# Two attention layers: head outputs compacted by DMA into two blocks of 96 rows, and maxima, exponentials and loads of x in other steps

## The chip, the cores and the metric

One core of a Trainium2 chip runs the whole program in one launch. The metric is device time in microseconds (us) from the program's start to its end. Engines that matter here: TensorE (PE, with its weight loads PEld), VectorE (DVE), ScalarE (ACT), GpSimd (POOL), and SyncE (SP), which issues the DMAs.

## What is computed

Four layers run one after the other on x of shape (16, 14, 14, 192): a GRU over the 196 positions, an attention layer (named l1 in the code), a layer of experts, and a second attention layer (l3). Each layer adds its output to its input, and its input is group-normalised first. Both attention layers have 12 heads of 16 channels, with a bias from relative positions, and differ in their weights only:

```python
q, k, v = (qkv[0], qkv[1], qkv[2])
attn = jnp.einsum('bqd,bkd->bqk', q * scale, k)
bias = rel_h[..., :, None] + rel_w[..., None, :]
attn = jax.nn.softmax(attn + bias.reshape(b * NH, h * w, h * w), axis=-1)
out = jnp.einsum('bqk,bkd->bqd', attn, v)      # then heads are put side by side: 192 channels
return out @ proj_w + proj_b
```

## The kernel before

`attention_layer` (L747) is called twice. B = 16 images of T = 196 tokens give N = 3136 columns; the 12 heads are worked as PAIRS = 6 pairs, and one item g of the main loop is one pair in one image, 96 items in all. A step n is two items, 2n and 2n+1; STEPS is 48 and LAG is 2.

**Main loop.** PE makes for each item the logits twice: `logits_by_query(g)` (L1115, queries on rows) into two PSUM banks, from which DVE takes the maxima of each row (`maxima`, L1327, one instruction per head), and `logits_by_key(g)` (L1129, keys on rows), to whose banks it then adds the negated maxima by a product with the unit matrix (L1136, after a wait for both maxima of the item). ACT takes the exponentials (L1280) of the sum. Two steps later `weigh_values` (L1151) multiplies them with v and a column of ones, and ACT and DVE copy the result of the even and the odd item to `o_quad` (`keep_even`, L1273, and `keep_odd`, L1320). In `o_quad` each head takes 32 rows: 16 of output, one of sums, 15 unused. So 12 heads fill three tiles of 128 rows. The order of PE in a step is: queries of 2n; values of step n-2; a piece `rel` of the relative positions where one is due (L1100 to L1102); queries of 2n+1; keys of 2n with its maxima; keys of 2n+1 with its maxima; a second `rel` where due. 16 of the 48 steps have one `rel`, 6 have two, 26 have none.

`logits_by_query` of the next item may write a bank as soon as DVE has taken that head's maxima of the item before. Its next use on PE stands behind the maxima product of item 2n+1, which waits for both maxima of that item.

**SP's order.** SP walks through `main_step(i)`, i = 0, 1, ..., one per item, in order, and each DMA waits in that order for what it needs: loads of q, k and rel for the next pair (`load`), stores for later quads, x for the residual (L984, eight loads at i = 55, 59, ..., 83), and for each eighth of the work h (one pair, eight images) the row of sums out to DRAM (`store_sums`, i = 12 + 8h), back as 98 rows of 32 (`load_sums`, i = 14 + 8h), and the reciprocals, split in a high and a low part by POOL, out again (`store_reciprocals`, i = 22 + 8h). DVE takes the reciprocals (L1332) at step n = 9 + 4h of its own program, so it stops there if the sums are not back.

**Tail.** After the loop the reciprocals of a half come back as 24 rows (`load_spread`, L962). Eight column tiles of 392 follow. For each: `spread_tile(n)` spreads the reciprocals over rows with a 0/1 matrix (L1202, three matmuls, one for each tile of 128 rows), DVE's `divide(n)` multiplies (L1371, three instructions), ACT makes the high part of all three blocks (L1296), POOL the low part (L1057), and PE projects with 2 x 9 matmuls (`product3`, L273): for two blocks of output rows, three input blocks with three terms each. DVE adds bias and residual (L1382, two instructions), in l1 also the moments for the next layer (L255, L259), and SP stores the tile (L1013). The spread tiles use one set of PSUM banks, so spread n waits for `divide(n-1)`; the projection waits for the low part. The tail's tiles lie where q was, so `load_spread(0)` waits for the last logits of the loop.

Of the kernel before, what the change touches and what calls it, by code (L numbers as in the profile page):

```python
# [7 lines left out]
ALU = mybir.AluOpType  # L8
# [718 lines left out]
class Ahead:  # L727
# [10 lines left out]
    def weights(self):  # L738
        at, parts = AT_W, []
        for dims in ((QUADS, CB, 128), (CB, C), (QUADS, CB, CP)):  # L740
            for part in range(2):
                parts.append(self.place(at, *dims, dt=f32r))
                at += int(np.prod(dims))
        return parts


def attention_layer(nc, tag, ins, x_in, y_out, qk_dram, rel_dram, sums_dram, rec_dram, given=None, kept=None, extra=(), taken=None, ahead=None, x_here=None, x_stored=None):  # L747
# [12 lines left out]
    with Scope(nc, tag) as s:  # L760
# [13 lines left out]
        for dims in ((QUADS, CB, 128), (CB, C), (28, 56), (QUADS, CB, CP)):  # L774
            w_raw.append(arena.place(at, *dims))
            at += int(np.prod(dims))
        pick_raw = arena.place(at, QUADS, 128)[:2 * HEADS]
        xy = arena.place(AT_QKA, CB, N)
        at, tail = AT_Q, []
        for part in range(3):  # L780
            tail.append(arena.place(at, 3 if part else 2, QUADS, TB, dt=f32r if part else f32))
            at += (3 if part else 2) * QUADS * TB
        hn, oh, ol = tail
        spread = arena.place(at, N, dt=f32r)[:2 * HEADS]
# [3 lines left out]
        for dims in ((QUADS, CB, 128), (CB, C), (QUADS, CB, CP)):  # L788
            if dims == (QUADS, CB, CP):
                at = AT_WO  # L790
# [9 lines left out]
        pick = s.sb("pick", [2 * HEADS, QUADS, 128], f32r)  # L800
# [26 lines left out]
        rec_ready, rec_high, rec_low, pick_ready = (s.sem(n) for n in "rec_ready rec_high rec_low pick_ready".split())  # L827
        spread_summed, hn_ready, oh_ready, ol_ready, y_summed, added, stored = (
# [44 lines left out]
        with nc.Block() as block:  # L873
            @block.sync
            def _(sp):
# [70 lines left out]

                def load_sums(h):
# [11 lines left out]
                def load_spread(half):  # L959
                    sp.wait_ge(rec_stored, 16 * (2 * PAIRS - 1 + half))  # L960
                    cols = slice(half * N // 2, (half + 1) * N // 2)
                    sp.dma_start(spread[:, cols].bitcast(f32), rec_dram[half].rearrange("a h n -> (a h) n").bitcast(f32)).then_inc(spread_in[half], 16)  # L962

                def main_step(i):
# [13 lines left out]
                    n = (i - 2 * B - 2 * len(REL_FIRST) - 1) // 4  # L978
                    if i == 2 * B + 2 * len(REL_FIRST) + 1 + 4 * n and 0 <= n < NT:
# [5 lines left out]
                    if i >= 12 and i % 8 == 4:  # L985
# [15 lines left out]
                for i in range(IMAGES + 2 * LAG + 1):  # L1001
# [7 lines left out]
                for place, source in extra:  # L1009
                    sp.dma_start(place, source).then_inc(extra_in, 16)  # L1010
                for m in range(NT):
                    sp.wait_ge(added, 2 * m + 2)
# [6 lines left out]
            def _(pool):  # L1019
# [33 lines left out]
                for n in range(NT):  # L1053
# [3 lines left out]
                    pool.tensor_tensor(ol[:, n % 3, :, :], hn[:, n % 2, :, :], oh[:, n % 3, :, :].bitcast(f32), ALU.subtract).then_inc(ol_ready, 1)  # L1057

            @block.tensor
            def _(pe):  # L1060
# [58 lines left out]
                def logits_by_key(g):  # L1119
# [4 lines left out]
                    both = unit[:TH, :].rearrange("p (a t) -> p a t", a=1).to_broadcast([TH, 2, TH])  # L1124
                    for head in range(2):
                        bank = ps[:TH, T_BANK + 2 * (g % 2) + head, :TB]
                        for half in range(2):
                            keys = slice(b * T + half * TH, b * T + (half + 1) * TH)
                            pe.matmul(bank[:, half * T:half * T + T], k[:, head, keys], q[:, head, queries],  # L1129
                                      start=half == 0, stop=False, skip_group_check=True)  # L1130
                    pe.wait_ge(max_ready, 2 * g + 2)
# [64 lines left out]
                def spread_tile(n):  # L1196
                    if n % (NT // 2) == 0:
                        pe.wait_ge(spread_in[n // (NT // 2)], 16)
                    if n >= 1:
                        pe.wait_ge(hn_ready, QUADS * n)  # L1200
                    for c in range(QUADS):
                        last = pe.matmul(ps[:, c, :TB], pick[:, c, :], spread[:, n * TB:(n + 1) * TB], start=True, stop=True)  # L1202
                    last.then_inc(spread_summed, 1)

                spread_tile(0)
                spread_tile(1)
                for n in range(NT):
                    if n + 2 < NT:
                        spread_tile(n + 2)
                    pe.wait_ge(ol_ready, n + 1)  # L1210
                    if n >= 2:
                        pe.wait_ge(added, 2 * n - 2)
                    for m in range(CB):
                        product3(pe, ps[:CP, 4 + 2 * (n % 2) + m, :TB], lambda c: woh[:, c, m, :], lambda c: wol[:, c, m, :],
                                 lambda c: oh[:, n % 3, c, :], lambda c: ol[:, n % 3, c, :], blocks=QUADS).then_inc(y_summed, 1)

            @block.scalar
            def _(act):
# [63 lines left out]
                for n in range(STEPS + LAG):  # L1282
                    if n >= LAG:
# [3 lines left out]
                    if n < STEPS:  # L1287
                        exponentials(2 * n)
                        exponentials(2 * n + 1)
                    if n in rel_second:  # L1290
                        rel(rel_second[n])
                for n in range(NT):
                    act.wait_ge(hn_ready, QUADS * n + QUADS)
                    if n >= 3:
                        act.wait_ge(y_summed, 2 * n - 4)
                    act.activation(oh[:, n % 3, :, :], hn[:, n % 2, :, :], ACT.Copy).then_inc(oh_ready, 1)  # L1296

            @block.vector
            def _(dve):
# [48 lines left out]
                for n in range(STEPS + LAG):  # L1348
# [10 lines left out]
                    if n >= 9 and n % 4 == 1:  # L1359
                        reciprocals((n - 9) // 4)  # L1360
# [1030 lines left out]
```

## Time and profile before

| what | us |
|---|---|
| median of 3 runs | 1670.99 (1663.61 to 1677.24) |
| the profiled execution | 1666.41 |
| its span, first to last instruction | 1664.6 |
| l1: main loop, tail | 641 to 844, 844 to 894 |
| l3: main loop, tail | 1414 to 1614, 1614 to 1664.6 |

The four times of stages are from the span's start. The profile is that of one execution. A timeline row gives the start, how long the merged instructions took together, the engine, the source line, the operation, the tiles and the count; in brackets stands how long the engine had been idle before, and what ended it. PEld rows are weight loads; their starts show when PE turned to the next matmuls. DVE and ACT work in their program's order, and so does SP.

### The profile page before, as it was taken

What the parts mean: (1) busy time and instruction counts of PE and PEld (TensorE: products, weight loads), DVE (VectorE), ACT (ScalarE), POOL (GpSimd) and SP (SyncE); (2) the same over time, 40 slices, a digit from 0 to 9 for tenths busy, and PEclk for the clock granted to TensorE, in tenths of its full rate; (3) what the DMA queues carried; (4) which work ended last, traced back from release to release, by engine and by line L of the source; (5) the groups of instructions that cost most, each with busy time, mean ns of one, the idle gap of its engine ahead of it and who ended that gap; (6) DMA issues with size and microseconds to landing.
All of it is one profiled execution on the core that took longest, in us unless ns stands there. A gap on an engine that the chain in (4) does not pass through costs nothing. (4 is left out here: it accounts for less than half of the span.)

```text
span 1664.6 us, 49731 instructions
## 1 busy us (share of the span) xinstructions
PE 1413.6 (85%) x19315; PEld 1204.8 (72%) x19315; DVE 1123.5 (67%) x3964; ACT 776.5 (47%) x1702; POOL 431.0 (26%) x686
## 2 busy tenths in 40 slices
PE   4958888888887688999976889979997869999988
PEld 4847777777776578878755657768886568777866
DVE  7867777777778855767656793544443774677764
ACT  3723333333334455656532532645555265556542
POOL 2722222222224501000032310356664041000005
PEclk9955555555555789999977579999999579999998
DMA  3000000000000256897815402423223456797932
GB/s 94 1 21 4 4 5 4 4 4 4 5 4 18 75 176 135 265 262 167 172 38 160 142 19 88 155 92 98 88 88 99 134 160 157 194 264 213 197 82 59
DMA packets 71588, 164.47 MB, mean 99 GB/s; under 512 B 17698, under 2 KB 42730, under 8 KB 68860
## 3 DMA queue, kind: packets, MB, share of 16 engines
q1 hardware_dynamic: 65980, 148.44, 33.1%
q0 software_dynamic: 5376, 12.85, 2.5%
q8 instruction: 156, 2.56, 0.6%
q14 instruction: 76, 0.62, 0.1%
HBM read 93.84 MB, written 67.42 MB: 97 GB/s over the span
## 5 line engine op out<-in xcount | busy, mean ns | idle before, releaser
L1327 DVE TENSOR_REDUCE l_mt<-l_ps 98x2 fp32r<-98x392 f32 x384 | 198.6, 559 | 102.1 <-PE l_ps L1115 99.7
L514 PE MATMUL gru_ps_r<-gru_hp,gru_wp 128*128 128x16 f16 x3920 | 200.0, 176 | 68.2 <-DVE gru_hp L489 68.2
L514 PEld LDWEIGHTS gru_ps_r<-gru_hp,gru_wp 128*128 128x128 f16 x3920 | 150.7, 106 | 88.5 <-DVE gru_hp L489 88.5
L1280 ACT ACTIVATE l_arena<-l_ps 98x784 f32<-98x784 f32 x192 | 158.4, 826 | 77.4 <-PE l_ps L1136 67.0
L514 PE MATMUL gru_ps_n<-gru_hp,gru_wp 128*128 128x16 f16 x3920 | 191.2, 174 | 0.0
L580 ACT ACTIVATE gru_reset<-gru_ps_r,gru_unscale 128x32 f32<-128x32 f32 x196 | 56.5, 288 | 216.8 <-PE gru_ps_r L514 216.8
L514 PEld LDWEIGHTS gru_ps_n<-gru_hp,gru_wp 128*128 128x128 f16 x3920 | 150.0, 104 | 0.0
L567 POOL TENSOR_TENSOR gru_kept<-gru_keep,l0s_state 128x32 f32<-128x32 f32 x196 | 49.6, 253 | 304.6 <-ACT gru_keep L582 304.6
L1115 PE MATMUL l_ps<-l_arena,l_arena 128*98 128x196 f32 x768 | 113.6, 267 | 5.2 <-DVE l_arena L1309 2.7
L1115 PEld LDWEIGHTS l_ps<-l_arena,l_arena 128*98 128x98 f32 x768 | 92.1, 167 | 27.9 <-DVE l_mt L1327 20.3
L1136 PE MATMUL l_ps<-l_unit,l_mt 98*98 98x196 f32 x768 | 110.7, 266 | 0.2 <-DVE l_mt L1327 0.2
L1043 POOL CAST l_rec_parts<-l_sums 98x32 fp32r<-98x32 f32 x24 | 5.1, 211 | 399.3 <-DVE l_sums L1332 352.2
L1129 PE MATMUL l_ps<-l_arena,l_arena 128*98 128x196 f32 x768 | 102.4, 256 | 0.0
L1247 ACT ACTIVATE l_arena<-l_ps 56x448 fp32r<-56x448 f32 x84 | 63.1, 751 | 69.4 <-PE l_ps L1102 68.1
L2191 DVE TENSOR_TENSOR l_arena<-mx_ps,l_arena 128x512 fp32r<-128x512 f32 x56 | 38.7, 692 | 81.7 <-ACT l_arena L1999 81.7
L1136 PEld LDWEIGHTS l_ps<-l_unit,l_mt 98*98 98x98 f32 x768 | 84.9, 166 | 9.6 <-DVE l_mt L1327 0.3
L1151 PE MATMUL l_ps<-l_arena,l_arena 98*32 98x196 f32 x1536 | 84.6, 338 | 1.2 <-DVE l_arena L1320 1.2
L1129 PEld LDWEIGHTS l_ps<-l_arena,l_arena 128*98 128x98 f32 x768 | 85.5, 166 | 0.0
L514 PE MATMUL gru_ps_z<-gru_hp,gru_wp 128*128 128x16 f16 x1960 | 81.1, 174 | 0.0
L1314 DVE TENSOR_TENSOR l_arena<-l_ps,l_arena 56x448 fp32r<-56x448 f32 x84 | 65.6, 782 | 20.1 <-ACT l_arena L1247 18.1
L1100 PE MATMUL l_ps<-l_arena,l_arena 128*56 128x224 f32 x168 | 58.4, 347 | 18.9 <-DVE l_arena L1314 15.9
L582 ACT ACTIVATE gru_keep<-gru_ps_z,gru_unscale 128x32 f32<-128x32 f32 x196 | 56.4, 288 | 37.6 <-PE gru_ps_z L514 37.6
(378 smaller groups left out, 4051.2 us busy)
## 6 DMA issues: line engine op xcount, KB each, us to landing
l_arena<-qk SPq DMA_DIRECT2D x96, 294.0 KB
qk<-l_arena SPq DMA_DIRECT2D x48, 392.0 KB, 6.0
rel<-l_arena SPq DMA_DIRECT2D x24, 686.0 KB
l_arena<-rel SPq DMA_DIRECT2D x48, 343.0 KB
qk<-l_arena SPq DMA_DIRECT2D x12, 784.0 KB, 6.8
l_arena<-in_experts_dram SPq DMA_DIRECT2D x8, 1152.0 KB, 7.4
l_arena<-x SPq DMA_DIRECT2D x24, 294.0 KB, 6.9
l_arena<-x SPq DMA_DIRECT2D x24, 196.0 KB, 2.9
```

What stands on the lines that cost most here:

```text
L514: last = pe.matmul(out[:, b, B * m:B * m + B], wp[:, wi, g, m, :], hp[:, b, part, B * k:B * k + B], start=False, stop=True, skip_group_che ...
L580: act.activation(reset[:, b, :], ps_r[:, b, :2 * B], ACT.Sigmoid, scale=unscale[:, 0:1]).then_inc(reset_ready, 1)
L582: act.activation(keep[:, b, :], ps_z[:, b, :2 * B], ACT.Sigmoid, scale=unscale[:, 0:1]).then_inc(keep_ready, 1)
L1100: pe.matmul(out, rh[:, n, :], line(high), start=True, stop=False)
L1115: last = pe.matmul(ps[:TH, S_BANK + head, half * T:half * T + T], q[:, head, queries], k[:, head, keys], start=True, stop=True)
L1129: pe.matmul(bank[:, half * T:half * T + T], k[:, head, keys], q[:, head, queries], start=half == 0, stop=False, skip_group_check=True)
L1136: last = pe.matmul(bank[:, :, half * TH:(half + 1) * TH], mt[:TH, g % 2, n:n + 1].to_broadcast([TH, TH]), both, start=False, stop=half == ...
L1151: last = pe.matmul(ps[row:row + 32, O_BANK, :T], v_flat[:TH, place:place + 32], probs[(2 * pair + odd) % SLOTS][:TH, head, keys * T:keys * ...
L1247: act.activation(rel_out(r, 0), rel_sums(r), ACT.Copy).then_inc(rel_high, 1)
L1280: act.activation(probs[g % SLOTS][:TH, :, :], banks, ACT.Exp).then_inc(p_ready, 1)
L1314: dve.tensor_tensor(rel_out(r, 64), rel_sums(r), rel_out(r, 0).bitcast(f32), ALU.subtract).then_inc(rel_low, 1)
L1327: dve.tensor_reduce(mt[:TH, g % 2, 2 * head:2 * head + 2], ps[:TH, S_BANK + head, :TB].rearrange("p (h k) -> p h k", h=2), AXIS.X, ALU.max ...
```

## The change

- **Compaction.** A new step on SP, `compact(h)`, copies for each eighth the 16 output rows of each of its two heads from `o_quad` to `o_rows`, two blocks of 96 rows (two DMAs of 16 rows x 6272 bytes each, 24 DMAs per layer). Those of h = 0 to 5 are issued at i = 58 to 63, those of h = 6 to 9 at i = 66, 74, 82, 90, the last two after the loop.
- **Tail on two blocks.** Spread, divide, high and low part and projection work on two blocks of 96 rows: per column tile 2 spread matmuls, 2 divides, 784 columns of high and low part, and 2 x 6 matmuls. The projection is one function that runs the eight matmuls that need only the high part, and then waits for the low part. Spread tiles alternate between two sets of banks.
- **Own homes.** `hn`, `oh`, `ol`, `spread` and `o_rows` lie where neither q nor live data lie, and the wait of `load_spread(0)` for the last logits is gone; `load_spread` waits for the compaction in its place. `load_spread(0)` is issued ahead of the last sums. The reciprocals of h = 10 are taken at step 47 in place of 49. In l1 the loads of constants for the next layer (`extra`) are issued after the divides, ahead of the last two stores.
- **Maxima and exponentials.** `subtract_maxima(g)` is cut out of `logits_by_key(g)`. That of the odd item 2n+1 now follows `logits_by_query(2n+2)` in the next step. On ACT the exponentials of the odd item go to the head of the next step too.
- **Loads of x** are issued at i = 85 to 92.

The weights of the projection and the 0/1 matrix get the matching shapes.

```diff
+        o_rows = arena.place(N, CB, N)[:CP]
+        oh, ol = (arena.place(at, 3, CB, TB, dt=f32r)[:CP] for at in (AT_REL, AT_QKB))
+        hn = [arena.place(at + 3 * CB * TB, CB, TB)[:CP] for at in (AT_REL, AT_QKB)]
+        spread = arena.place(3 * N, N, dt=f32r)[:2 * HEADS]
...
+                def compact(h):
+                    p, half = divmod(h, 2)
+                    if h == 0:
+                        sp.wait_ge(rel_stored, 64 * QUADS)
+                    sp.wait_ge(even_kept, 4 * (h + 1))
+                    sp.wait_ge(odd_kept, 4 * (h + 1))
+                    cols = slice(half * N // 2, (half + 1) * N // 2)
+                    for head in range(2):
+                        row, at = 64 * (p % 2) + 32 * head, 2 * HD * (p % 3) + HD * head
+                        sp.dma_start(o_rows[at:at + HD, p // 3, cols], o_quad[p // 2][row:row + HD, cols]).then_inc(compacted, 16)
...
-                    n = (i - 2 * B - 2 * len(REL_FIRST) - 1) // 4
-                    if i == 2 * B + 2 * len(REL_FIRST) + 1 + 4 * n and 0 <= n < NT:
+                    n = i - (PAIRS - 1) * B - 5
+                    if 0 <= n < NT:
...
+                    if 58 <= i < 64:
+                        compact(i - 58)
+                    if i >= 66 and i % 8 == 2 and i < IMAGES:
+                        compact(6 + (i - 66) // 8)
...
+                compact(2 * PAIRS - 2)
                 store_reciprocals(2 * PAIRS - 2)
+                load_spread(0)
+                store_sums(2 * PAIRS - 1)
                 load_sums(2 * PAIRS - 1)
-                sp.wait_ge(t_summed, IMAGES)
-                load_spread(0)
+                compact(2 * PAIRS - 1)
                 store_reciprocals(2 * PAIRS - 1)
                 load_spread(1)
...
                 for n in range(STEPS + LAG):
                     if n < STEPS:
                         logits_by_query(2 * n)
+                    if 1 <= n <= STEPS:
+                        subtract_maxima(2 * n - 1)
                     if n >= LAG:
                         weigh_values(n - LAG)
...
                         logits_by_query(2 * n + 1)
                         logits_by_key(2 * n)
+                        subtract_maxima(2 * n)
                         logits_by_key(2 * n + 1)
...
+                def project(n):
+                    outs = [ps[:CP, 4 + 2 * (n % 2) + m, :TB] for m in range(CB)]
+                    pe.wait_ge(oh_ready, n + 1)
...
+                    pe.wait_ge(ol_ready, n + 1)
...
                 spread_tile(0)
                 spread_tile(1)
+                pe.wait_ge(even_kept, STEPS)
+                pe.wait_ge(odd_kept, STEPS)
+                for n in range(NT):
+                    project(n)
+                    if n + 2 < NT:
+                        spread_tile(n + 2)
...
+                    if n == STEPS - 1:
+                        reciprocals(2 * PAIRS - 2)
                 reciprocals(2 * PAIRS - 1)
```

## Rows read from the trace of the kernel before

**Rows 1.** Windows: stretch, length, busy time of engines (instructions), PE clock, DMA share, GB/s.

```profile
1550.00:1570.00 20.00, 19.78 (x227) 15.94 (x219) 14.31 (x31) 10.76 (x18) 0.47 (x2) 1.00 1.03 194
1590.00:1614.00 24.00, 23.42 (x283) 18.69 (x281) 16.00 (x34) 13.86 (x21) 0.93 (x4) 1.00 0.25 52
...
1626.00:1628.00 2.00, 2.00 (x6) 1.45 (x7) 0.81 (x2) 0.91 (x1) 1.72 (x2) 0.50 0.00 0
```

**Rows 2.** Timeline of l3, one step without rel: start, us, engine, line.

```profile
1604.75 0.44 PEld L1115 LDWEIGHTS l_ps<-l_arena,l_arena 128*98 128x98 f32 x4
...
1606.10 0.53 PEld L1115 LDWEIGHTS l_ps<-l_arena,l_arena 128*98 128x98 f32 x4 [0.31 <-DVE l_mt L1327]
...
1606.56 0.44 PEld L1129 LDWEIGHTS l_ps<-l_arena,l_arena 128*98 128x98 f32 x4
...
1606.92 0.44 PEld L1136 LDWEIGHTS l_ps<-l_unit,l_mt 98*98 98x98 f32 x4
...
1607.29 0.44 PEld L1129 LDWEIGHTS l_ps<-l_arena,l_arena 128*98 128x98 f32 x4
...
1607.85 0.43 PEld L1136 LDWEIGHTS l_ps<-l_unit,l_mt 98*98 98x98 f32 x4
...
1608.21 0.45 PEld L1115 LDWEIGHTS l_ps<-l_arena,l_arena 128*98 128x98 f32 x4
...
1608.76 1.04 DVE L1327 TENSOR_REDUCE l_mt<-l_ps 98x2 fp32r<-98x392 f32 x2 [0.96 <-PE l_ps L1115]
```

**Rows 3.** Timeline of l3, the same place of a step with one rel.

```profile
1448.46 0.44 PEld L1129 LDWEIGHTS l_ps<-l_arena,l_arena 128*98 128x98 f32 x4
...
1448.99 0.44 PEld L1136 LDWEIGHTS l_ps<-l_unit,l_mt 98*98 98x98 f32 x4
```

**Rows 4.** Timeline around reciprocals of h = 6: the sums out, DVE's wait in l3, and in l1.

```profile
1549.91 0.55 SPq L945 DMA_DIRECT2D sums<-l_arena  x2
...
1563.54 0.36 DVE L1332 RECIPROCAL l_sums<-l_sums 98x32 f32<-98x32 f32 x1 [1.19 <-DMA l_sums<-sums]
...
792.23 0.35 DVE L1332 RECIPROCAL l_sums<-l_sums 98x32 f32<-98x32 f32 x1 [3.03 <-DMA l_sums<-sums]
```

**Rows 5.** Timeline of l3 from the loop's last copy to the tail's first divides.

```profile
1614.23 0.36 DVE L1320 COPY l_arena<-l_ps 64x196 f32<-64x196 f32 x1 [1.07 <-PE l_ps L1151]
...
1617.15 0.29 SPq L962 DMA_DIRECT2D l_arena<-rec  x1
1617.75 0.35 DVE L1332 RECIPROCAL l_sums<-l_sums 98x32 f32<-98x32 f32 x1 [2.77 <-DMA l_sums<-sums]
...
1619.88 1.31 PE L1202 MATMUL l_ps<-l_arena,l_pick 24*128 24x392 f32 x3 [5.71 <-DMA l_arena<-rec]
...
1621.23 1.51 DVE L1371 TENSOR_TENSOR l_arena<-l_ps,l_arena 128x392 f32<-128x392 f32 x3 [3.13 <-PE l_ps L1202]
```

**Rows 6.** Timeline of l3's tail: low part, high part, spread and projection of a tile, last addition.

```profile
1626.99 2.71 POOL L1057 TENSOR_TENSOR l_arena<-l_arena,l_arena 128x1176 fp32r<-128x1176 f32 x1 [0.28 <-ACT l_arena L1296]
...
1628.73 1.19 ACT L1296 ACTIVATE l_arena<-l_arena 128x1176 fp32r<-128x1176 f32 x1 [1.82 <-DVE l_arena L1371]
...
1640.33 0.80 PE L1202 MATMUL l_ps<-l_arena,l_pick 24*128 24x392 f32 x3
...
1641.06 3.45 PE L273 MATMUL l_ps<-l_arena,l_ahead 128*96 128x392 f32 x18
...
1644.43 0.80 PE L1202 MATMUL l_ps<-l_arena,l_pick 24*128 24x392 f32 x3
...
1659.19 0.62 DVE L1382 SCALAR_TENSOR_TENSOR l_arena<-l_ps,l_small,l_arena 96x392 f32<-96x392 f32 x1 [0.99 <-PE l_ps L273]
```

**Rows 7.** Timeline of DVE in l1's tail: divides, additions and moments of a tile, the end.

```profile
873.37 1.47 DVE L1371 TENSOR_TENSOR l_arena<-l_ps,l_arena 128x392 f32<-128x392 f32 x3
...
874.77 1.31 DVE L1382 SCALAR_TENSOR_TENSOR l_arena<-l_ps,l_small,l_arena 96x392 f32<-96x392 f32 x2
...
893.80 0.38 DVE L259 BATCH_NORM_AGGREGATE to_moments<-l_arena 96x2 f32<-96x6 f32 x4
```

More of the change, by code:

```diff
@@ L739, in weights @@
         at, parts = AT_W, []
-        for dims in ((QUADS, CB, 128), (CB, C), (QUADS, CB, CP)):
+        for dims in ((QUADS, CB, 128), (CB, C), (CB, CB, CP)):
             for part in range(2):
@@ L773, in attention_layer @@
         w_raw, at = [], AT_QKB
-        for dims in ((QUADS, CB, 128), (CB, C), (28, 56), (QUADS, CB, CP)):
+        for dims in ((QUADS, CB, 128), (CB, C), (28, 56), (CB, CB, CP)):
             w_raw.append(arena.place(at, *dims))
             at += int(np.prod(dims))
-        pick_raw = arena.place(at, QUADS, 128)[:2 * HEADS]
+        pick_raw = arena.place(at, CB, CP)[:2 * HEADS]
         xy = arena.place(AT_QKA, CB, N)
[L779 to L784, printed above, removed]
+        o_rows = arena.place(N, CB, N)[:CP]
+        oh, ol = (arena.place(at, 3, CB, TB, dt=f32r)[:CP] for at in (AT_REL, AT_QKB))
+        hn = [arena.place(at + 3 * CB * TB, CB, TB)[:CP] for at in (AT_REL, AT_QKB)]
+        spread = arena.place(3 * N, N, dt=f32r)[:2 * HEADS]
         rh, rl = arena.place(AT_REL, 28, 56, dt=f32r), arena.place(AT_REL + 28 * 56, 28, 56, dt=f32r)
@@ L1198, in spread_tile @@
                         pe.wait_ge(spread_in[n // (NT // 2)], 16)
[L1199 to L1202, printed above, removed]
+                    if n >= 2:
+                        pe.wait_ge(hn_ready, CB * (n - 1))
+                    for c in range(CB):
+                        last = pe.matmul(ps[:CP, 2 * (n % 2) + c, :TB], pick[:, c, :], spread[:, n * TB:(n + 1) * TB], start=True, stop=True)
                     last.then_inc(spread_summed, 1)
[L1205 to L1210, printed above, removed]
+                def project(n):
+                    outs = [ps[:CP, 4 + 2 * (n % 2) + m, :TB] for m in range(CB)]
+                    pe.wait_ge(oh_ready, n + 1)
                     if n >= 2:
@@ L1213, in _ @@
                     for m in range(CB):
-                        product3(pe, ps[:CP, 4 + 2 * (n % 2) + m, :TB], lambda c: woh[:, c, m, :], lambda c: wol[:, c, m, :],
-                                 lambda c: oh[:, n % 3, c, :], lambda c: ol[:, n % 3, c, :], blocks=QUADS).then_inc(y_summed, 1)
+                        for c in range(CB):
+                            pe.matmul(outs[m], woh[:CP, c, m, :], oh[:, n % 3, c, :], start=c == 0, stop=False, skip_group_check=True)
+                            pe.matmul(outs[m], wol[:CP, c, m, :], oh[:, n % 3, c, :], start=False, stop=False, skip_group_check=True)
+                    pe.wait_ge(ol_ready, n + 1)
+                    for m in range(CB):
+                        for c in range(CB):
+                            last = pe.matmul(outs[m], woh[:CP, c, m, :], ol[:, n % 3, c, :], start=False, stop=c == CB - 1, skip_group_check=True)
+                        last.then_inc(y_summed, 1)
+                spread_tile(0)
+                spread_tile(1)
+                pe.wait_ge(even_kept, STEPS)
[4 more added lines that the diff above has]
+                        spread_tile(n + 2)
             @block.scalar
@@ L1282, in _ @@
                 for n in range(STEPS + LAG):
+                    if 1 <= n <= STEPS:
+                        exponentials(2 * n - 1)
                     if n >= LAG:
```

53 lines of the change are left out of this document (28 added, 25 removed).

## The prediction

> **What bounds the kernel now.** I read the page's slices first, to find the stages that the change touches: the two main loops, some 200 us each, and the two tails, some 50 us each. The rest of the program (GRU, experts) is untouched. Then the windows by stage: in the loop's second half PE is busy in 19.78 of 20 us at full clock, so PE's order of work sets the step, but the DMA share there is 1.03 at 194 GB/s, and only in the last pair does it fall to 0.25 [rows 1]. So two things lie close together in the loop, PE and the queue of DMAs. Then the timeline of one step, to see whether PE's busy time is work or waits. A step without rel takes 1604.75 to 1608.21, 3.46 us. A free block of four matmuls takes 0.36 to 0.37 us from its first weight load to the next block's (1606.56 to 1606.92 to 1607.29). Two blocks take longer: 1606.10 to 1606.56 is 0.46, and 1607.29 to 1607.85 is 0.56. These are waits for maxima, 0.09 + 0.19 = 0.28 us in a step, and DVE in its turn stands idle for 0.96 us until PE brings the next queries [rows 2]. Each waits for the other: the maxima product of item 2n+1 needs DVE's last maxima, and DVE's next maxima need queries that PE has put behind that product.
>
> Then the waits of DVE for the sums: at h = 6 it stops for 1.19 us in l3 and 3.03 us in l1, because the sums, issued at 1549.91, come back only at 1563.5 [rows 4]. Alone, the same round takes from 1614.6 to 1617.75 [rows 5]. The rest is queueing.
>
> Last the tail. In l3 a column tile takes 1640.33 to 1644.43, 4.10 us, all PE: 0.73 for three spread matmuls, 3.37 for 18 projection matmuls, 0.187 each [rows 6]. In l1 DVE is as full: divides (1.40 up to the additions' start), additions and moments fill the same 4.10 us [rows 7]. Ahead of it stand 5.7 us in which PE has no work, and the clock falls: at 1626 to 1628 it is 0.50 (the lower of the two levels, 1.2 GHz), with six projection matmuls in 2.00 us, 0.33 each [rows 1, 5].
>
> **The change, part by part: the loop.** With queries(2n+2) ahead of the odd maxima product, DVE gets its next input while it still works: each of the two banks is free as soon as that head's maxima are taken. A step holds two items of 1.04 us of maxima and one copy of 0.36 on DVE, 2.5 us with gaps [rows 2, 5], under PE's 3.18, so PE would wait no more, and a step takes 3.46 - 0.28 = 3.18 us. In a step with one rel the wait at the same place is 1448.46 to 1448.99, 0.53 - 0.37 = 0.16 us [rows 3]; I take that away too. In the six steps with two rel the order round the rel stays as it is, since PE, DVE and PE again hand the one rel bank on; I take 0. Moving ACT's exponentials costs nothing: two of them and a copy fill about 2 us of its step (13.86 us busy in 24 [rows 1]). Gross gain per layer: 26 x 0.28 + 16 x 0.16 = 9.8 us. It could be 0, if another wait takes its place; 9.8 is the upper bound.
>
> What the loop gives back: ten of the twelve copies of `compact(0..5)` stand ahead of `load_sums(6)` in SP's order, four of them ahead of `store_sums(6)`. Each moves 100 KB. No copy of this kind is in the trace. Lower bound: its bytes at the queue's 194 GB/s [rows 1], 0.52 us. Upper bound: as if each held the queue for the whole time of a lone transfer of 24 such rows, 1617.15 to 1619.88, 2.7 us [rows 5]. I take 0.52, since the copies are queued behind one another and share the latency. Ten cost 5.2 us; two loads of x that stood there (301 KB each, 1.55 us at the same rate) go, 3.1. So the sums of h = 6 come 2.1 us later, and DVE comes earlier by the loop's gain since the store of rel that SP has to wait for at i = 55, six and a half steps of 0.28, 1.8. Since DVE already waits there in both layers [rows 4], all 3.9 us are added. Net gain of a loop: 9.8 - 3.9 = 5.9 us, both 11.8. The other sums have room, and better room without the loads of x, which move to the stretch with a DMA share of 0.25 [rows 1]: 2.4 MB at 194 GB/s is 12 us, between i = 85 and the sums of h = 10. I cost them at nothing; if that stretch is too short, the last sums are a few us late and with them the tail.
>
> A rule that speaks against the change: the Trainium skill, "SBUF — State Buffer", section "Door 1: The DMA port swizzle", says that a transfer's rate goes with the SBUF ports that its partitions reach, and 16 neighbouring rows reach four of sixteen, at 27.2 GB/s each. An estimate by that page is 0.92 us a copy, which would make the ten 9.2 us and the whole 8 us slower than my sum.
>
> **The gap before the tail.** Of the wait at the loop's end, `load_spread(0)` goes ahead of the loop's last sums: the reciprocals of h = 10, now taken at step 47, can be back by about 1616.5. But DVE's program still has the reciprocals of h = 11 ahead of `divide(0)`, and their sums come at 1617.75 as before, as they start from the last copy at 1614.23 [rows 5]. So `divide(0)` starts at 1618.15 and not at 1621.23: 3.1 us, in each layer. What is late next is the sums, not the spread.
>
> **The tail of l3.** Per column tile: 12 x 0.187 + 2 x 0.243 = 2.74 us of PE in place of 4.10. DVE needs 2 x 0.5 + 2 x 0.62 = 2.3, POOL two thirds of 2.71, 1.81, ACT two thirds of 1.19, 0.8 [rows 6, 7]. So PE still sets the pace. A tile's way from its spread to its low part is 1.05 + 0.85 + 1.85 = 3.75 us, under the other tile's work (2.74) and the eight matmuls (1.5) that no longer wait for POOL. Start: divide 1618.15, high part done at 1620.0, first projection at the low clock 12 x 0.33 = 4.0, spread 0.9, so 1624.9. Then five tiles of 2.74, two projections of 2.25, 1643.1; I add 1.0 for a second tile partly at the low clock, 1644.1. The last additions take 0.9, and the end follows the last addition by 4.8 (1659.81 to 1664.6 [rows 6]): 1649.8. Gain 14.8 us, 3.1 of it the gap. If the clock stays low for two more tiles, it is 4.5 less.
>
> **The tail of l1.** Here DVE gets the bound: 0.95 for two divides, 1.25 additions, 1.45 moments (4.10 less 1.40 and 1.25), 3.65 us in place of 4.10 [rows 7]. After the first two slow tiles `divide(3)` starts at about 859; from there five divides, seven additions and eight moments are 4.8 + 8.8 + 11.6 = 25.2 us, end at 884.2 in place of 894.2. Gain 10.0 us.
>
> **The sum.** 14.8 + 10.0 + 11.8 = 36.6 us off the profiled execution's 1666.4 makes 1629.8. The median of the runs is 4.6 above that execution; I carry half of it and say 1632. The rest of the change (smaller weights, the other matrix) is off every path that I found.
>
> **Rivals.**
> 1. The copies are hidden wholly, as DMAs of other rows leave room, and the loops keep 9.8 each: 1666.4 - 24.8 - 19.6 + 2 = 1624. For it: the queue already lost two loads of x there. Against: DVE waits for that queue today [rows 4].
> 2. The copies are dearer than their bytes. At 1.0 us each the ten are 10.0, the loop gives back 8.7 and keeps 1.1: 1641. At 1.6 each it gives back 14.7 and a loop is 4.9 longer than before: 1653. For it: few rows to a transfer. Against: 16 rows are one for each of the 16 DMA engines. The rule quoted above is of this kind.
> 3. The loop's new order gains nothing, as a wait of PE for ACT or DVE takes the place, and only the tails gain: DVE would come no earlier, so the loops lose the 2.1 each, 1666.4 - 24.8 + 4.2 + 2 = 1648.
> 4. Not faster: the copies hold the queue like lone transfers, at 2.7 us each. Then each layer stops for 27 - 3.1 + 1.8 = 25.7 us at h = 6, and the whole is 1666.4 - 24.8 + 2 x (25.7 - 9.8) + 2 = 1675. It decides from 2.5 us a copy; slower by 1% wants 3.4. Against: nothing in the trace shows transfers in line that don't overlap; 1549.91 to 1563.5 holds two transfers of sums with loads of q, k, rel and x between them, and all of it takes 13.6 us [rows 4].
>
> **Chances.** My forecast, both mechanisms as costed: 0.55, own range 1622 to 1640. Rival 1: 0.16. Rival 2: 0.17. Rival 3: 0.08. Rival 4: 0.04. The range that leaves out no more than 2 in 10 goes from a little under rival 1 to the upper end of rival 2: 1614 to 1655. About 1% (17 us) is what a measurement of this kernel can tell from no change. Faster by more than that (under 1654) are the forecast, rivals 1 and 3, and rival 2 but for its end: 0.94; within 1%: 0.04, rival 4 and that end; slower: 0.02.
>
> **What would show it.** In the profile of the changed kernel: steps of the last pair at 3.18 us with DVE's idle time before maxima gone; `compact` landing at some 0.5 us each in the burst; a longer stop of DVE at the reciprocals of h = 6 (5 us in l3, 7 in l1); `divide(0)` some 3.9 us after the loop's last copy in place of 7.0; a column tile of 2.74 us in l3 and 3.65 in l1; the first projection at 0.33 us a matmul. I am wrong if DVE's stop at h = 6 is over 12 us, if loads of q and k come so late that PE waits for them, or if the clock stays at the lower level through the tails.

## The result and the profile after

The changed kernel takes 1659.1 us (median of 20 runs, 1638.7 to 1669.8), the kernel before beside it 1669.3 (20 runs, 1656.6 to 1677.2). The ratio is 0.993, 95% interval 0.991 to 0.995: faster by some 10 us, where 37 were forecast. The profiled execution took 1658.8, its span is 1656.9 (before: 1666.4 and 1664.6). "After" is the changed kernel alone; its runs lie 31 us apart, and that will matter. All stages below are those of one profiled execution of each kernel.

By stages, a loop being from its first maxima to the start of its last copy, and a tail from there to its end:

| stage | before | after | change | forecast |
|---|---|---|---|---|
| l1 loop | 641.46 to 844.35 | 643.14 to 843.24 | -2.8 | -5.9 |
| l1 tail | to 894.18 | to 883.38 | -9.7 | -10.0 |
| l3 loop | 1415.58 to 1614.23 | 1404.89 to 1605.48 | +1.9 | -5.9 |
| l3 tail | to 1664.6 | to 1656.9 | +1.0 | -14.8 |

What lies ahead of l1's loop, which the change doesn't touch, is 1.7 us longer in this execution.

The loop's steps came out as costed. Timeline of after, l3, weight loads of PE: the same block of two steps without rel, one after the other (queries of the odd item, behind the values).

```profile
1591.38 0.43 PEld L1134 LDWEIGHTS l_ps<-l_arena,l_arena 128*98 128x98 f32 x4 [0.31 <-DVE l_mt L1364]
...
1594.56 0.43 PEld L1134 LDWEIGHTS l_ps<-l_arena,l_arena 128*98 128x98 f32 x4 [0.31 <-DVE l_mt L1364]
```

1591.38 to 1594.56 is 3.18 us, in place of 3.46 [rows 2]. A step with one rel took 4.36, as costed (4.52 - 0.16). Now DVE in l3. The reciprocals (L1369 now) wait for the sums: the first row is that of h = 1, the second of h = 6, the fourth of h = 11, with the first divide behind it. The third is the maxima of a step without rel.

```profile
1467.51 0.35 DVE L1369 RECIPROCAL l_sums<-l_sums 98x32 f32<-98x32 f32 x1 [2.42 <-DMA l_sums<-sums]
...
1556.87 0.35 DVE L1369 RECIPROCAL l_sums<-l_sums 98x32 f32<-98x32 f32 x1 [7.30 <-DMA l_sums<-sums]
...
1593.38 1.04 DVE L1364 TENSOR_REDUCE l_mt<-l_ps 98x2 fp32r<-98x392 f32 x2 [0.43 <-PE l_ps L1134]
...
1610.87 0.35 DVE L1369 RECIPROCAL l_sums<-l_sums 98x32 f32<-98x32 f32 x1 [5.03 <-DMA l_sums<-sums]
1611.26 1.04 DVE L1409 TENSOR_TENSOR l_arena<-l_ps,l_arena 96x392 f32<-96x392 f32 x2
```

DVE's wait for queries fell from 0.96 to 0.43 us [rows 2], but it stops for 7.30 us at h = 6, where it stopped for 1.19, and in l1 for 7.58 in place of 3.03 [rows 4]. PE stands behind it, and something follows that I had not costed: its clock falls. Timeline of PE, then windows (columns as in [rows 1]) of after around this stop, and of the tails.

```profile
1557.70 1.11 PE L1134 MATMUL l_ps<-l_arena,l_arena 128*98 128x196 f32 x4 [6.45 <-DVE l_mt L1364]
1558.61 0.87 PE L1147 MATMUL l_ps<-l_arena,l_arena 128*98 128x196 f32 x4
1559.28 0.87 PE L1157 MATMUL l_ps<-l_unit,l_mt 98*98 98x196 f32 x4
...
1617.46 0.96 PE L1226 MATMUL l_ps<-l_arena,l_pick 24*96 24x392 f32 x2
...
1622.52 0.96 PE L1226 MATMUL l_ps<-l_arena,l_pick 24*96 24x392 f32 x2
```

```profile
1550.00:1553.00 3.00, 1.25 (x21) 0.68 (x19) 0.00 (x0) 1.36 (x3) 0.00 (x0) 1.00 1.00 157
1553.00:1556.00 3.00, 0.00 (x0) 0.00 (x0) 0.00 (x0) 0.00 (x0) 0.00 (x0) 0.81 1.06 211
1556.00:1558.00 2.00, 0.30 (x2) 0.31 (x2) 1.13 (x3) 0.00 (x0) 0.46 (x2) 0.50 1.05 179
1558.00:1560.00 2.00, 2.00 (x13) 1.94 (x13) 1.51 (x4) 0.00 (x0) 0.00 (x0) 0.50 1.07 185
1560.00:1562.00 2.00, 2.00 (x17) 1.89 (x20) 0.75 (x2) 0.82 (x1) 0.00 (x0) 0.57 0.93 138
1562.00:1564.00 2.00, 2.00 (x30) 1.61 (x30) 1.37 (x4) 1.15 (x2) 0.00 (x0) 1.00 0.86 171
...
1618.00:1630.00 12.00, 12.00 (x35) 8.44 (x34) 5.62 (x11) 2.06 (x3) 3.71 (x2) 0.50 0.18 50
...
1640.00:1650.00 10.00, 10.00 (x31) 7.73 (x30) 4.15 (x8) 1.49 (x2) 3.73 (x2) 0.50 0.23 66
...
857.00:859.00 2.00, 2.00 (x8) 1.49 (x7) 0.15 (x1) 0.00 (x0) 1.87 (x1) 0.61 0.50 133
859.00:861.00 2.00, 2.00 (x11) 1.59 (x12) 1.52 (x4) 0.46 (x1) 0.00 (x0) 1.00 0.09 26
```

While PE stood for 6.45 us the granted clock went from 1.00 to 0.50 (2.4 to 1.2 GHz), and its next matmuls, four in 0.87 us in place of 0.53, ran at the lower level until about 1561.7 (the window from 1560 has a mean of 0.57). In l3's tail the clock is 0.50 from the first projection to the end, with PE busy all the time: a column tile takes 1617.46 to 1622.52, 5.06 us, where 2.74 were forecast and 4.10 were taken before [rows 6]. In l1 the same tail starts as low, but at about 858.6 the clock rises (0.61 is the mean of 857 to 859), and there a tile takes 3.46 us, set by DVE as forecast.

### The profile page after: what moved, and what is told of

It is laid out like the page before. It is cut to its first block and busy times, and to the rows that moved or that the text cites. A ratio compares the mean times of both kernels' runs of the same rounds, so it can differ in the third digit from the quotient of the medians.

```text
span 1656.9 us, 49568 instructions
## 1 busy us (share of the span) xinstructions
PE 1393.6 (84%) x19203; PEld 1189.6 (72%) x19203; DVE 1113.6 (67%) x3948; ACT 770.7 (47%) x1702; POOL 415.4 (25%) x686
## 3 DMA queue, kind: packets, MB, share of 16 engines
q1 hardware_dynamic: 67516, 153.03, 35.6%
## 5 line engine op out<-in xcount | busy, mean ns | idle before, releaser
L1157 PE MATMUL l_ps<-l_unit,l_mt 98*98 98x196 f32 x768 | 104.4, 259 | 0.0
```

What stands on the lines that cost most here:

```text
L1157: last = pe.matmul(bank[:, :, half * TH:(half + 1) * TH], mt[:TH, g % 2, n:n + 1].to_broadcast([TH, TH]), both, start=False, stop=half == ...
```

## The experiments

Three theories of the missing 27 us: the clock in l3's tail (16 us, as 7 tiles x 2.32); the sums, which come later as the queue of DMAs is fuller (stops, and what the clock loses behind them); the new order, which might gain nothing. All times below are medians, each beside runs of the kernel before on the same chip. A run that is set beside another or beside after can be from another chip. Each diff shows its main lines only.

**Matmuls of no use in the pause.** After, with PE kept busy where it waits for the spread and for the first high part, in both layers; their results are written over.

```diff
+                warm(14)
                 spread_tile(0)
                 spread_tile(1)
+                warm_after(14)
                 pe.wait_ge(even_kept, STEPS)
```

> The changed kernel with 28 matmuls added per layer that compute nothing for the output (14 between the loop's last matmul and the first spread, 14 between the second spread and the first projection, each 96 x 96 weights on 392 columns). Theory 'clock': the l3 tail of the changed kernel runs its eight tiles at granted clock 0.50, 5.06 us each, only because PE had little work for 8 us ahead of it. With PE kept at work the tiles take 2.7 to 3.0 us from the first or second on, so l3's tail (51.4 us from the loop's last copy to the end) falls by 12 to 16 us, l1's (40.1) by 0 to 3, and the whole by 12 to 18 us. Rival 'shape': blocks of 96 rows in 392 columns are slow as such, or the tiles wait for POOL or DVE; then a tile stays at about 5 us in l3 and the whole is 0 to 3 us slower for the added matmuls.

Measured: 1637.8 us (1636.7 to 1641.7), before 1670.3; ratio 0.981 (0.978 to 0.984), 21 us less than after. Windows of this kernel in l3's tail:

```profile
1606.00:1608.00 2.00, 2.00 (x12) 1.58 (x10) 1.58 (x4) 0.15 (x1) 0.46 (x2) 1.00 0.87 101
...
1614.00:1616.00 2.00, 2.00 (x11) 1.34 (x10) 1.31 (x3) 0.21 (x1) 1.72 (x1) 1.00 0.14 40
...
1620.00:1630.00 10.00, 10.00 (x52) 7.50 (x50) 7.38 (x15) 2.58 (x3) 7.15 (x4) 1.00 0.34 98
```

The clock stays at 1.00; 52 matmuls stand in ten microseconds where there were 31. A column tile takes 2.84 us in place of 5.06, and the tail 1601.2 to 1636.9, 35.7 us in place of 51.4. Nothing of the tail's own work was changed, so the clock was the cause of those 15.7 us (but for 0.2 of a shorter gap), and the theory that the tiles are slow as such is out. l1's tail is 3.8 us shorter, more than the 0 to 3 expected. The four runs lie 5 us apart, where after's twenty lie 31 apart.

**The copies of h = 0 to 5 spread out.**

```diff
-                    if 58 <= i < 64:
-                        compact(i - 58)
+                    if 63 <= i < 75 and i % 2 == 1:
+                        compact((i - 63) // 2)
```

> The changed kernel with the copies of h = 0 to 5 at i = 63, 65, 67, 69, 71, 73 in place of 58 to 63, so that none of them stands ahead of the sums of h = 6. Theory 'burst': DVE's stop at the reciprocals of h = 6 (7.6 us in l1, 7.3 in l3) falls to 2 to 4 us, and with it the stretch of lower clock behind it, so the whole gains 2 x (4 to 6) = 8 to 12 us. Rival 'the faster loop': the stop comes from the queue as it is and DVE coming earlier; then it stays over 6 us in both layers, or moves to h = 7, and the whole stays within 3 us.

Measured: 1654.9 us (1645.7 to 1666.1), ratio 0.992 (0.989 to 0.996), the same as after. Timeline of its DVE in l3, h = 6 and h = 7:

```profile
1557.92 0.35 DVE L1369 RECIPROCAL l_sums<-l_sums 98x32 f32<-98x32 f32 x1 [1.93 <-DMA l_sums<-sums]
...
1575.22 0.35 DVE L1369 RECIPROCAL l_sums<-l_sums 98x32 f32<-98x32 f32 x1 [5.06 <-DMA l_sums<-sums]
```

The stop went with the copies, to h = 7; in l1 too (1.08 and 5.16). So the copies cause most of it, and the queue has to carry them somewhere, as the rival had it; the loops take 201.2 and 198.2 us where after's take 200.1 and 200.6. This profile also shows the other outcome of l3's tail, with the tail's code as in after, and in its last row l1's tail:

```profile
1614.00:1618.00 4.00, 0.76 (x5) 0.41 (x4) 2.33 (x5) 1.02 (x2) 0.64 (x3) 0.62 0.50 61
1618.00:1622.00 4.00, 4.00 (x13) 3.12 (x13) 0.00 (x0) 0.69 (x1) 3.49 (x2) 0.53 0.13 38
1622.00:1630.00 8.00, 8.00 (x41) 6.07 (x41) 5.95 (x12) 2.40 (x3) 3.72 (x2) 1.00 0.26 74
...
865.00:870.00 5.00, 5.00 (x15) 3.50 (x15) 3.48 (x13) 0.86 (x1) 1.89 (x1) 0.50 0.22 62
```

In l3 the clock rises at 1622, after the first projection, as I had assumed in the sum, and the tail takes 35.9 us (1611.42 to 1647.3). In l1 it is the other way round than in after: the clock stays at 0.50 until about 884, and that tail takes 47.2 us in place of 40.1. So each of the two tails can go either way. The ten runs of this kernel fall into five from 1645.7 to 1651.1 us, with a mean granted clock of 0.783 to 0.789, and five from 1658.7 to 1666.1 with 0.770 to 0.779. That fits two outcomes of a tail, but only one of these executions has a profile. A median of such a kernel depends on how often each outcome came.

**The order of maxima and exponentials, taken back and alone.** First after with the old order on PE and ACT, then before with the new order only.

```diff
-                    if 1 <= n <= STEPS:
-                        subtract_maxima(2 * n - 1)
...
                         logits_by_key(2 * n + 1)
+                        subtract_maxima(2 * n + 1)
```

> The changed kernel with the order of maxima products and exponentials of the kernel before, all else as changed. Theory: steps without rel go back from 3.18 to 3.46 us and with one rel from 4.36 to 4.52; DVE comes later to the sums, so its stop at h = 6 is 1.5 to 2 us shorter; per layer 9.8 - 2 = 7 to 8 us longer, the whole +14 to +16. Rival 'the stop eats it': what the order gains ahead of a stop is lost at the stop, since the sums' way through the queue sets that time; only steps behind h = 6 (14 of 0.28 us, 3.9) are lost, and the whole is +5 to +8 us.

Measured: 1666.7 us (1646.8 to 1677.8), ratio 0.995 (0.992 to 0.999). The order is worth 7.6 us by the medians and 4 by the ratios to before, whose intervals overlap; in the profiles the loops are 6.0 (l1) and 3.6 us (l3) longer than after's. That is not 14 to 16, and near the rival's 5 to 8. Timeline of its DVE at h = 6, in l1 and l3:

```profile
794.31 0.35 DVE L1367 RECIPROCAL l_sums<-l_sums 98x32 f32<-98x32 f32 x1 [5.43 <-DMA l_sums<-sums]
...
1563.66 0.35 DVE L1367 RECIPROCAL l_sums<-l_sums 98x32 f32<-98x32 f32 x1 [4.98 <-DMA l_sums<-sums]
```

Here DVE comes no earlier than in before, so what the stops are longer than before's, 2.4 and 3.8 us, is the part of the copies less the two loads of x that went.

```diff
+                    if 1 <= n <= STEPS:
+                        subtract_maxima(2 * n - 1)
...
                         logits_by_key(2 * n)
+                        subtract_maxima(2 * n)
                         logits_by_key(2 * n + 1)
```

> The kernel before with nothing changed but the order of maxima products and exponentials. Theory: 26 steps lose 0.28 us and 16 lose 0.16, 9.8 us a layer, less 1.5 to 2.5 us of longer stops at h = 1, 5, 6: -14 to -17 us over both layers. Rival 'the stop eats it, with the clock': the stops grow by what the steps gain, PE idles, the clock falls behind each; then -4 to -8 us.

Measured: 1661.3 us (1660.2 to 1666.4), ratio 0.996 (0.994 to 0.997): 7 us less than before by the ratio, 9 by the medians, where the theory had 14 to 17 and the rival 4 to 8. Timeline of its DVE in l3, h = 1 and h = 6:

```profile
1478.96 0.35 DVE L1338 RECIPROCAL l_sums<-l_sums 98x32 f32<-98x32 f32 x1 [2.70 <-DMA l_sums<-sums]
...
1565.10 0.35 DVE L1338 RECIPROCAL l_sums<-l_sums 98x32 f32<-98x32 f32 x1 [4.02 <-DMA l_sums<-sums]
```

With no copy in the program, the faster steps alone raise the stops from 1.10 to 2.70 at h = 1 and from 1.19 to 4.02 at h = 6. DVE comes earlier, the sums don't. These two stops give back 4.4 of the 9.8 us in l3, and 2.1 in l1 (0.61 to 1.96 and 3.03 to 3.75). The loops themselves are 6.2 us (l1) and 1.0 us (l3) shorter than before's in the profiles.

**The same dummy matmuls in the kernel before** (of 384 columns).

```diff
+                dummies(14)
                 spread_tile(0)
                 spread_tile(1)
+                dummies(14)
```

> The kernel before with the same two groups of 14 matmuls of no use, of 384 columns here, in both layers, one ahead of the first spread and one between the second spread and the first projection. Nothing of the output changes. Theory (the changed kernel alone has a tail that can stay at the lower level, because its tile keeps less work for TensorE; before rises by itself in its second tile): only the first projection of each layer changes, 18 x (0.33 - 0.187) = 2.6 us a layer at most, 5 us in all, 1663 to 1669 against before's 1669. Rival (dummy matmuls are worth some 20 us in any tail with such a pause, so that the gain of the changed kernel with them says nothing of the change): 1645 to 1655.

Measured: 1667.4 us, before 1670.5; ratio 1.000 (0.997 to 1.002). The number is the theory's, but the run shows less than I meant it to. Windows:

```profile
1618.00:1622.00 4.00, 0.79 (x3) 0.47 (x3) 1.51 (x4) 0.00 (x0) 0.46 (x2) 1.00 0.27 61
1622.00:1626.00 4.00, 3.59 (x10) 2.89 (x11) 1.86 (x4) 1.85 (x2) 2.35 (x1) 0.54 0.05 20
...
1630.00:1650.00 20.00, 20.00 (x104) 16.01 (x102) 13.41 (x25) 5.95 (x5) 12.02 (x5) 1.00 0.22 61
```

The second spread there waits for the first divides, so the second group comes too late to fill the pause, and the clock falls all the same. It was at 1.00 again by 1630, where it was by 1632 in the profile of before, without dummies. So the dummies are not worth 20 us wherever they stand; what a held clock would give before was not tried.

**The reciprocals one step later** (after with the dummy matmuls).

```diff
-                    if n >= 9 and n % 4 == 1 and n < STEPS:
-                        reciprocals((n - 9) // 4)
+                    if n >= 10 and n % 4 == 2 and n < STEPS:
+                        reciprocals((n - 10) // 4)
```

> The changed kernel with the matmuls of no use, and with VectorE's reciprocals of each pair of heads one step later in its program (steps 10, 14, ... in place of 9, 13, ...). Theory (the stops at h = 6 and h = 1 come of too little slack for the way of the sums there and back, and a step of 3.2 to 4.4 us more covers it): the stops of h = 1 go, those of h = 6 fall from 7.0 to about 3.5 us, with half of the time at the lower clock behind them, 2 x (3.5 + 2 + 1) = 13 us less than the kernel with the matmuls alone: 1622 to 1628. Rival (the queue decides; what VectorE no longer waits for is waited for by the scaled values or the next store, since the queue's order is the same): under 4 us, 1634 to 1638.

Measured: 1638.0 us (1631.5 to 1646.9, four runs), ratio 0.983 (0.979 to 0.986): no gain over the dummies alone that can be told. In its profile (1631.5) the stops of h = 1 are gone, those of h = 6 are 3.33 (l1) and 4.02 (l3), l1 has a new one of 4.25 at h = 10, and the loops are 2.7 and 2.4 us shorter than with the dummies alone. The mechanism is seen, its worth is not settled by these runs.

**All of it**: dummies, later reciprocals, spread copies, and the sums of h = 11 ahead of `load_spread(0)`. Only the last is new and shown.

```diff
-                load_spread(0)
                 store_sums(2 * PAIRS - 1)
                 load_sums(2 * PAIRS - 1)
+                load_spread(0)
```

> The changed kernel with the matmuls of no use, the reciprocals one step later, the copies of h = 0 to 5 one every two images from image 63, and in front of the tail the store and the load of the sums of h = 11 ahead of the load of the spread. Theory (all the losses found have a slack or an order as their cause): no stop of VectorE over 2 us in the loops, the first divide of a tail 4 us behind the loop's last copy in place of 4.5 and 5.8, some 3 to 6 us less than with the reciprocals alone: 1617 to 1624. Rival (one lot of work on one queue; the stop moves to h = 7 or to the last sums): no faster than with the reciprocals alone, 1624 to 1632.

Measured: 1635.4 us (1630.7 to 1639.1), ratio 0.980 (0.977 to 0.983): no gain over the dummies alone that can be told, and not the 1617 to 1624 expected. The sums of h = 11 came back sooner, 3.6 us behind the last copy in place of 5.2, but then the first divide waited for the spread. And a stop of 3.64 us at h = 10, just ahead of the loop's end, brought the clock down into the tail:

```profile
1591.00:1594.00 3.00, 3.00 (x18) 2.08 (x11) 0.37 (x1) 0.33 (x1) 0.00 (x0) 0.50 0.26 34
...
1604.00:1606.00 2.00, 2.00 (x11) 1.56 (x10) 0.00 (x0) 0.00 (x0) 0.00 (x0) 0.88 0.00 0
```

The tail took 39.4 us in place of 35.7. On SP six loads of x stand close ahead of the sums of h = 10, which took from 1581.64 to the load's issue at 1587.94, 6.3 us. I had costed these loads at nothing; the next two runs test that.

**Half of the loads of x behind the loop**, first with the dummies alone, then with later reciprocals and spread copies too. `load_x(n)` is one load of x.

```diff
-                    if 0 <= n < NT:
+                    if 0 <= n < 4:
...
                 load_spread(1)
+                for n in range(4, NT):
+                    load_x(n)
```

> The changed kernel with the matmuls of no use, and the loads of x for the tiles 4 to 7 after the load of the spread's second half in place of images 89 to 92; tiles 0 to 3 as before. Theory (the loads of x, costed at nothing in the prediction, hold up the sums of h = 10, whose way there and back is 5.6 us, and with them the copies, the scaled values and the tail's first tile): the way of the sums of h = 10 takes 3 us, no stop of VectorE on them, and from the loop's last copy in l3 to the first divide 4.5 us in place of 5.5; the time 1 to 3 us less than the kernel with the matmuls alone, 1635 to 1637, and no wait of the additions for x. Rival (the last sums wait for the load of the spread and not for x, or x now comes too late for tile 4): way of the sums of h = 10 still over 5 us or additions that wait for a DMA, 1638 to 1642.

> The changed kernel with the matmuls of no use, the reciprocals one step later, the copies of h = 0 to 5 one every two images from image 63, and the loads of x for the tiles 4 to 7 behind the loop; the load of the spread stays ahead of the last sums. Theory (in the run with all of it, the stop of 3.6 us on the sums of h = 10 brought the clock down just ahead of the tail, which cost it 4 us; with those loads gone the stop goes): no stop of VectorE over 3 us in the loops, the clock at 1.00 at the loop's end, the l3 tail 36 us: 1624 to 1630. Rival (the stop at the loop's end is the late reciprocals' own, since a step later is as late again for the copies behind it): stop of over 3 us at h = 10 still there, 1631 to 1637.

Measured: 1658.8 us (ratio 0.995, 0.992 to 0.999), and 1648.6 (1633.0 to 1649.6, four runs; ratio 0.987, 0.980 to 0.993). Both are worse than the same without it (1637.8 with the dummies alone, 1635.4 with all of it), and neither theory had that; the rival of the first had x come too late, but only for tile 4, and at 1638 to 1642 us. The one profile of the first is of its slowest execution (1687.0 us, mean granted clock 0.70); there too DVE's third divide waits for x, 8.69 us. Timeline of the second: SP around the sums of h = 10, then DVE and PE at the third divide.

```profile
1590.14 0.68 SPq L944 DMA_DIRECT2D sums<-l_arena  x2
...
1592.88 0.31 SPq L961 DMA_DIRECT2D l_sums<-sums  x1
...
1613.18 1.03 DVE L1424 TENSOR_TENSOR l_arena<-l_ps,l_arena 96x392 f32<-96x392 f32 x2 [8.84 <-DMA l_arena<-x]
...
1615.42 0.61 PE L1241 MATMUL l_ps<-l_arena,l_ahead 96*96 96x392 f32 x1 [4.86 <-DVE l_arena L1435]
```

```profile
1612.00:1616.00 4.00, 0.58 (x2) 0.56 (x3) 2.82 (x6) 0.86 (x1) 0.82 (x1) 0.59 0.04 9
...
1620.00:1630.00 10.00, 10.00 (x29) 7.04 (x28) 4.20 (x8) 1.72 (x2) 3.77 (x2) 0.50 0.20 58
```

The theory's part on the sums holds: from the store of the sums of h = 10 to the load behind it takes 2.74 us, and with all loads of x ahead it took 1590.91 to 1596.99, 6.08, in the kernel with the dummies alone. But DVE's program waits for all eight loads of x ahead of its third divide. It stood 8.84 us, PE 4.86, and the clock went to 0.50 for the rest of the tail, dummies or not. One of the four runs took 1633.0 us all the same, and it has no profile.

**The loads of x ahead of the last copies, and DVE's wait behind the third divide.** The second kernel of the last experiment (dummies, later reciprocals, spread copies, x for tiles 0 to 3 as there), with two things changed together: where x for tiles 4 to 7 is loaded, and where DVE waits for x. The diff shows these against after.

```diff
                 load_sums(2 * PAIRS - 1)
+                for n in range(4, NT):
+                    load_x(n)
                 compact(2 * PAIRS - 1)
...
                 divide(1)
-                dve.wait_ge(x_in_again, 16 * NT)
...
                         divide(n + 2)
+                    if n == 0:
+                        dve.wait_ge(x_in_again, 16 * NT)
```

> As the kernel before this in the study (matmuls of no use, reciprocals a step later, copies of h = 0 to 5 spread from image 63), with the loads of x for the tiles 4 to 7 right behind the load of the sums of h = 11, ahead of the last copies, and VectorE's wait for all of x behind its third divide in place of ahead of it. Theory (what made the two kernels with late loads of x slow was that wait: VectorE stood 8.8 us for x, TensorE 4.9 us behind it, and the clock went to the lower level for the rest of the tail): no wait of VectorE for x over 1 us, the clock at 1.00 through both tails, the way of the sums of h = 10 under 3 us: 1624 to 1631. Rival (the loads now hold up the copies of h = 11 and the spread's second half, and TensorE stops at tile 4): 1635 to 1650.

Measured: 1619.0 us (1616.1 to 1623.1), before 1668.9; ratio 0.971 (0.968 to 0.973). It beats both kernels, by 40 us the one after, and the 1624 to 1631 expected. Timeline of its DVE, then a window of its tail in l3:

```profile
1588.15 0.35 DVE L1384 RECIPROCAL l_sums<-l_sums 98x32 f32<-98x32 f32 x1 [3.58 <-DMA l_sums<-sums]
...
1593.97 1.03 DVE L1424 TENSOR_TENSOR l_arena<-l_ps,l_arena 96x392 f32<-96x392 f32 x2 [3.45 <-PE l_ps L1231]
```

```profile
1600.00:1610.00 10.00, 10.00 (x52) 7.65 (x51) 7.80 (x16) 3.37 (x4) 6.32 (x4) 1.00 0.42 121
```

DVE waits for PE at its third divide, not for x. The stops of DVE in the loops are 2.41 us (l1, h = 7) and 1.02 (l3, h = 6), the loops take 192.7 and 189.8 us (after: 200.1 and 200.6), the first divide of l3 comes 4.3 us behind the last copy, and that tail takes 34.5. The 40 us are those of the five edits together, of which the dummies alone gave 21; the two new edits were not parted.

## Why the prediction was wrong

The direction was right, by mechanisms that the profile shows; 27 us of the size were not there. No rival has the measured time either: 1659 lies between rival 2's upper end and rival 4. The forecast's -36.6 against -7.6 in the profiled executions is 29 us, by its steps:

- **The tail of l3, 15.8 us: the step that failed.** "I add 1.0 for a second tile partly at the low clock": the whole tail was at it. From the first divide to the end the forecast has 31.65 us and after took 45.6, so 14.0 of the 15.8 are the clock. The rest of that chain was right: in the profile with spread copies, where the clock rises after the first projection as the sum has it, the same way takes 31.5 us. (That the whole tail of the run with the dummies, 35.7, is so near the forecast 35.6 is luck: its first projection is at the full clock, which the sum didn't have, and its gap is 1.6 us longer than forecast.) I knew that the clock was at 0.50 at the tail's start [rows 1] and took from the trace of before that it rises in two tiles; that was one execution's outcome, and of a tail in which PE had more to do. In the prediction "the clock stays at the lower level through the tails" stands among what would make it wrong; it had no chance and no price beyond two tiles.
- **The gap before the tail, in that sum and l1's.** "their sums come at 1617.75 as before" failed: the sums of h = 11 now stand behind `load_spread(0)` on SP, and in l3 behind sums of h = 10 that the loads of x had held up (a way of 1595.14 to 1600.70 there). The gap went from 7.0 to 5.8 us in l3 and from 6.85 to 4.5 in l1, a gain of 1.2 and 2.3 in place of 3.1.
- **The loops, 11.0 us for the two.** The gross gain came, and the give-back was too small. The starts of DVE's copies of odd items (one in each step) part the two. Away from h = 1 and h = 6 the loops of after are 8.9 us (l1) and 7.7 us (l3) shorter; the two steps at h = 1 are 0.7 and 2.5 us longer, the three at h = 6 are 5.4 and 7.1 us longer. For l1 that makes 8.9 - 0.7 - 5.4 = 2.8 us gained, for l3 7.7 - 2.5 - 7.1 = -1.9, as measured. A step without a stop gains 0.29 us there, so the gross gain is about 10.4 and 9.1 (forecast 9.8), and what h = 6 takes back is 6.3 and 8.0, where "all 3.9 us are added" was the term. The stop itself grew by 4.6 and 6.1; the rest, about 1.8 in each, is my estimate of what PE lost at the lower clock behind it, a cost put at nothing. "The other sums have room" failed at h = 1, where DVE had waited in before too (0.61 and 1.10): 1.3 us in l1 and 3.1 in l3, of which the longer stop is 1.1 and 1.3; the granted clock of 0.69 in 1468 to 1472 stands behind the rest in l3.
- **The price of a copy.** The stops of after exceed the forecast by 0.7 and 2.2 us over ten copies, which makes 0.59 and 0.74 us a copy if all of that is theirs. With the old order, where DVE's earlier coming plays no part, 2.4 and 3.8 us and the 3.1 of the two loads of x make 0.55 and 0.69. So a copy cost an estimated 0.55 to 0.75 us, not 0.52. The rule of the Trainium skill that the prediction weighed ("SBUF — State Buffer", section "Door 1: The DMA port swizzle") gave 0.92 as an estimate: above what these runs show, and in the right direction. By these estimates rival 2, with 1.0 us and more a copy, is out.
- **The loads of x, costed at nothing.** Not nothing: 6.08 us for a round of sums that takes 2.74 without them.
- **The tail of l1** came out at -9.7 for -10.0, with a tile of 3.46 set by DVE for the forecast 3.65. Part of that is luck: the clock rose there in time, and in the profile with spread copies, where it didn't, the same tail takes 47.2 us, a gain of 2.6.

Of the rivals, 2 at 1.0 us a copy comes nearest to the loops of after by its number (a loop keeps 1.1 us; after's keep 0.4 on the mean), but not by its mechanism: the copies are cheaper than that, and the rest goes to the clock and to h = 1. Rival 3 (the new order gains nothing) is out: the steps are shorter, and DVE, which comes earlier, loses part of that waiting for the sums.

Open is why the clock in a fully busy tail rises in one execution and not in the next, with the same instructions in the tail, and how often it does so in after: its runs at 1638.7 and 1646.8 us have no profile.

## What to carry to other kernels

When a change takes work from an engine behind a pause in which its clock falls, cost the whole stage at the lower level as a rival of its own, with a chance; here that was 14 us, about half of the error. When a step gets faster, every round through memory that had just enough slack turns into a stop, so list the rounds with their slack before counting the gain. And when a load moves into a quiet stretch, look for the small transfer behind it in the queue's order, and for the one wait in a program that stands for all of the loads.

## What the runs showed of the hardware

- A stop of PE of 6.45 us inside a loop at full clock brought the granted clock to 0.50, and it was 1.00 again by 1562, about 4 us after PE had gone on (l3, h = 6); in l1 it took 6.5 us after a stop of 6.72. A stop of 1.57 us at h = 1 in l3 had the same effect: 0.69 as the mean of 1468 to 1472. One of 0.88 us at h = 1 in l1 did not: 1.00 throughout.
- l3's tail of after, with PE busy 12.00 of 12.00 us from 1618 to 1630, stayed at 0.50 from the first projection to the last, 1613.3 to 1651, while in another execution the clock rose after the first projection of the same code. The Trainium skill, "TensorE: Matmul & The Clock Gate", section "Part 1: The HAM clock gate", says that the lower level is the default and activity releases it. By the busy share of PE in these profiles, l1's tail of after (1.00 from about 858.6) and l3's of the run with spread copies (from 1622) agree; l3's tail of after does not, and l1's of the run with spread copies does not (0.50 until about 884). Matmuls of no use ahead of the tail kept it at 1.00 in the run with the dummies alone (1606 to 1630), but not where PE had stopped for 3.08 us just ahead of them (0.50 in 1591 to 1594, with all of it) or stopped behind them for 4.86 (late loads of x).
